# Who scales and rounds the ternary weights: six passes over 128x2048 moved from VectorE to GpSimd

## The reference

```python
weights = softmax(tokens @ gate_w); topk_w, topk_idx = top_k(weights, 2)
e0 = silu(x @ w0.T + b0);  e1 = silu(x @ w1.T + b1)
out = e0 * topk_w[:, 0] * (topk_idx[:, 0] == 0) + e1 * topk_w[:, 1] * (topk_idx[:, 1] == 1)
```

```python
scale = 1.0 / clip(mean(abs(w)), 1e-05)
wq = clip(round(w * scale), -1.0, 1.0) / scale
```

## Time and profile before

| what | value |
| --- | --- |
| median of 3 runs | 1935.88 us (1935.24 to 1936.64) |
| the profiled execution | 1937.66 us, of which the span of the trace is 1935.7 us |
| mean granted TensorE clock of that execution | 0.971 of full speed |
| busy shares of the span | PE 93%, DVE 73%, ACT 53%, POOL 26% |

### The profile page before, as it was taken

One profiled execution on the slowest core, in us unless ns is written; L12 is line 12 of the kernel. 1 busy time (PEld: TensorE's weight loads), 2 busy tenths in 40 slices (PEclk: granted clock), 3 DMA queues, 4 the chain that ended last, 5 costly groups with the idle time before them and its releaser, 6 DMA issues. The chain is left out here.

```text
span 1935.7 us, 33792 instructions
## 1 busy us (share of the span) xinstructions
PE 1793.0 (93%) x11747; PEld 1585.4 (82%) x11750; DVE 1410.4 (73%) x3157; ACT 1020.4 (53%) x2247; POOL 507.4 (26%) x531
## 2 busy tenths in 40 slices
PE   7958999999999999999967999999969999999698
PEld 6637999999898989899845888888857888888587
DVE  6478787777777787778666566666777777777786
ACT  4344656555556555565535565556622666666421
POOL 0514030211203030302011233333441444343342
PEclk9978999999999999999988999999989999999799
DMA  4011000000000000000021112110000000000011
GB/s 160 1 77 33 2 4 9 2 10 0 11 0 11 0 12 0 3 0 1 1 98 49 53 58 64 47 64 14 9 1 17 15 9 23 9 10 4 23 56 40
DMA packets 17591, 48.43 MB, mean 25 GB/s; under 512 B 2602, under 2 KB 7347, under 8 KB 15796
## 3 DMA queue, kind: packets, MB, share of 16 engines
q1 hardware_dynamic: 16596, 45.99, 7.3%
q10 hardware_dynamic: 864, 0.83, 0.1%
HBM read 45.89 MB, written 0.92 MB: 24 GB/s over the span
## 5 line engine op out<-in xcount | busy, mean ns | idle before, releaser
L1280 ACT ACTIVATE a_pH<-banks 125x512 fp32r<-125x512 f32 (+1 forms) x384 | 203.9, 544 | 273.6 <-PE banks L195 192.2
L1351 DVE TENSOR_TENSOR a_pL<-banks,a_pH 125x512 fp32r<-125x512 f32 (+1 forms) x384 | 235.2, 623 | 100.3 <-ACT a_pH L1280 96.6
L1854 POOL TENSOR_TENSOR a_prob<-a_prob,a_rinv 112x750 f32<-112x750 f32 x128 | 184.1, 1438 | 395.9 <-DVE a_rinv L2157 395.9
L1327 DVE TENSOR_SCALAR_CACHE_REDUCE a_prob<-banks 128x500 f32<-128x500 f32 x336 | 223.1, 677 | 18.0 <-PE banks L195 9.0
L1181 PE MATMUL banks<-ident,a_prob 128*125 128x128 f32 x1344 | 201.6, 274 | 6.6 <-ACT a_prob L1265 4.4
L195 PE MATMUL banks<-a_pH,a_head_vH 125*128 125x256 f32 (+1 forms) x576 | 203.2, 353 | 2.1 <-DVE a_pL L1351 1.1
L1265 ACT ACTIVATE a_prob<-a_prob,a_nmax 128x1000 f32<-128x1000 f32 x168 | 188.0, 1122 | 28.2 <-DVE a_nmax L1330 28.2
L1181 PEld LDWEIGHTS banks<-ident,a_prob 128*125 128x125 f32 x1344 | 187.1, 188 | 10.0 <-ACT a_prob L1265 4.9
L1137 POOL TENSOR_TENSOR a_head_oH<-a_o,ones 128x256 fp32r<-128x256 f32 (+1 forms) x24 | 16.5, 687 | 625.5 <-DVE a_o L1360 625.5
L195 PE MATMUL banks<-a_pH,a_head_vL 125*128 125x256 f32 (+1 forms) x576 | 173.0, 300 | 0.0
L195 PE MATMUL banks<-a_pL,a_head_vH 125*128 125x256 f32 (+1 forms) x576 | 172.8, 300 | 0.0
(11 more groups left out here) (422 smaller groups left out, 5094.9 us busy)
## 6 DMA issues: line engine op xcount, KB each, us to landing
a_w_out<-in_f_out SPq DMA_DIRECT2D x6, 1024.0 KB, 4.8
a_w_in<-in_f_in SPq DMA_DIRECT2D x12, 512.0 KB, 4.7
f_raw<-in_f_w SPq DMA_DIRECT2D x9, 513.0 KB, 3.6
pair_qk_raw<-in_a_qk SPq DMA_DIRECT2D x16, 256.0 KB, 2.7
f_quant_raw<-in_f_w SPq DMA_DIRECT2D x3, 1024.0 KB, 7.5
a_head_w_raw<-in_a_w SPq DMA_DIRECT2D x8, 384.0 KB, 3.0
a_v<-in_ctx_rows SPq DMA_DIRECT2D x4, 576.0 KB, 7.5
f_w_out<-in_f_out SPq DMA_DIRECT2D x2, 1024.0 KB, 5.1
```

The lines of the kernel that those rows point to most:

```text
L1280: act.activation(pH[:, c % RING, 0:wide], TB[c % 4][0:KB, 0:wide], ACT.Copy).then_inc(t_high, 1)
L1327: dve.tensor_scalar(prob[:, at, c * CHUNK:(c + 1) * CHUNK], SB[c % 3][:, 0:CHUNK], SCALE, None, ALU.mult, ALU.max, accum_out=chunk_max[:, ...
L1351: dve.tensor_tensor(pL[:, c % RING, 0:wide], TB[c % 4][0:KB, 0:wide], pH[:, c % RING, 0:wide].bitcast(F32), ALU.subtract).then_inc(t_done, 1)
L1854: pool.tensor_tensor(both, both, rinv[:, n % RING, :].unsqueeze(2).to_broadcast([SEQ, 2, KEYS]), ALU.mult).then_inc(p_normed, 1)
```

## The change

The six passes over `quant_raw` leave VectorE's loop and stand at the end of GpSimd's block of the same stage, as scale 0, round 0, scale 1, round 1, scale 2, round 2. Shapes, types, operations, semaphores and their counts are as before; ScalarE's and TensorE's blocks are not touched.

```diff
-        def quant_scale(dve, m):
-            dve.wait_ge(scale_ready, 1)
-            dve.tensor_scalar(quant_raw[:, m, :], quant_raw[:, m, :], w_scale[:, m:m + 1], 1.0,
+        def quant_scale(pool, m):
+            pool.wait_ge(scale_ready, 1)
+            pool.tensor_scalar(quant_raw[:, m, :], quant_raw[:, m, :], w_scale[:, m:m + 1], 1.0,
                               ALU.mult, ALU.min).then_inc(quant_scaled, 1)
...
-            dve.wait_ge(quant_scaled, m + 1)
-            dve.tensor_scalar(quant_raw[:, m, :], quant_raw[:, m, :], -1.0, MAGIC, ALU.max, ALU.add).then_inc(quant_clipped, 1)
+            pool.wait_ge(quant_scaled, m + 1)
+            pool.tensor_scalar(quant_raw[:, m, :], quant_raw[:, m, :], -1.0, MAGIC, ALU.max, ALU.add).then_inc(quant_clipped, 1)
...
             pool.wait_ge(w_cut, 1)
             pool.tensor_tensor(wL[:], w_raw[:], wH[:].bitcast(F32), ALU.subtract).then_inc(w_cut, 1)
+            for m in range(3):
+                quant_scale(pool, m)
+                quant_round(pool, m)
...
                     dve.reciprocal(w_scale[:], s.w_mean[:]).then_inc(scale_ready, 1)
-                if QUANT_AT < i <= QUANT_AT + 3:
-                    quant_scale(dve, i - QUANT_AT - 1)
-                if QUANT_AT + 1 < i <= QUANT_AT + 4:
-                    quant_round(dve, i - QUANT_AT - 2)
```

More of the change, by code:

```diff
@@ L710, in layer0_ffn, with quant_round @@
         EB = B[4:8]
-        def quant_scale(dve, m):
-            dve.wait_ge(scale_ready, 1)
-            dve.tensor_scalar(quant_raw[:, m, :], quant_raw[:, m, :], w_scale[:, m:m + 1], 1.0,
+        def quant_scale(pool, m):
+            pool.wait_ge(scale_ready, 1)
+            pool.tensor_scalar(quant_raw[:, m, :], quant_raw[:, m, :], w_scale[:, m:m + 1], 1.0,
                               ALU.mult, ALU.min).then_inc(quant_scaled, 1)
-        def quant_round(dve, m):
-            dve.wait_ge(quant_scaled, m + 1)
-            dve.tensor_scalar(quant_raw[:, m, :], quant_raw[:, m, :], -1.0, MAGIC, ALU.max, ALU.add).then_inc(quant_clipped, 1)
+        def quant_round(pool, m):
+            pool.wait_ge(quant_scaled, m + 1)
+            pool.tensor_scalar(quant_raw[:, m, :], quant_raw[:, m, :], -1.0, MAGIC, ALU.max, ALU.add).then_inc(quant_clipped, 1)
         block = ctx.enter_context(nc.Block())
```

## The result

| | median of 5 runs | range |
| --- | --- | --- |
| before | 1935.88 us | 1933.40 to 1938.09 |
| after | 1966.31 us | 1963.64 to 1970.99 |

The ratio is 1.0168, with a 95% interval of 1.0152 to 1.0183; of 1935.88 us that is 32.5 us more (29.4 to 35.4); the two medians as they stand are 30.4 us apart. The forecast was 2.6 us more, and its range ended at 1950. The profiled execution of the changed kernel took 1963.64 us, the lowest of its five.

What follows compares the result with a forecast made beforehand. The stage's end, ScalarE's last brought_back at 143.52, was taken as the bound; 134.9 + 6 d with d = 1.87 gave 146.1, so 1935.88 + 2.6 = 1938.5 us, range 1936.3 to 1950.

Steps and rivals of the forecast that it cites:

- The price of one pass, d: Length of each scale or round on GpSimd over 2048 columns: 1.87 us, range 1.87 to 4.45.
- GpSimd's loop is slower than a copy's: Rival, chance 0.38: the six GpSimd passes run well above 1.87 us each; 13.4 us later at 3.66, 18.1 at 4.45.
- The sum: Stage end at 134.9 + 6 d = 146.1 against 143.52, that is 6 d - 8.6 = 2.6 us later.
- the start: GpSimd's scale 0 starts at about 131.35, after the reciprocal ending at 130.95 and an addition ending at 131.31.
- the additions: VectorE's additions let in between GpSimd's passes, three at 0.5 us each, added to GpSimd's end.
- The reload: Library reload on GpSimd, in its idle stretch ahead of the six passes, put at nothing.
- The rival of the first call: Rival, chance 0.03: GpSimd's first pass behind the reload pays about 6 us for loading code, giving 1944.5 us.
- a sign of being wrong: The prediction called itself wrong if, among other signs, GpSimd's first pass was longer than the third.
- The lock: VectorE instructions with two SBUF operands stand still while GpSimd computes, entering only where GpSimd's next instruction waits for a semaphore.
- The cap on a gain: ScalarE's chain, ending at about 141.1 at best, limits any gain at the stage's end to 2.4 us or 0.12%.
- The tails: Behind GpSimd's last round: ScalarE's last brought_back to 146.05 and VectorE's four remaining additions to 146.15.

Runs made afterwards that it cites:

- prices: Kernel before plus a stage of its own with fifteen GpSimd instructions: multiply and add 1.90 us, multiply alone 5.4, multiply and minimum 7.09; its total time was not read.
- forms: Kernel before plus a stage of its own with GpSimd in other operation pairs, then small VectorE instructions beside GpSimd ones; rows read, not its time; addition stood 3.7 of 5.4 us.
- one_op: Changed kernel with one operation in each of the six passes, limits at -1 and 1 left out: 1959.67 us, ratio 1.0134.
- madd: Changed kernel with all six passes as multiply and add with plain numbers, so no ternary weights come out: 1936.50 us, ratio 1.0013.
- rounds_pool: Half of the change: VectorE keeps the three scales, GpSimd does only the three rounds: 1953.00 us, ratio 1.0098 against the kernel before.
- no_passes: Kernel before without the six passes on any engine, and brought_back not waiting for them: 1931.16 us, ratio 0.9982.
- fast_form: Change rebuilt: GpSimd multiplies by the scale and adds the rounding constant, VectorE takes maximum and minimum: 1937.22 us, ratio 1.0019 against the kernel before.
- spread: Kernel before rebuilt: scales on ScalarE and VectorE, VectorE writes bf16, no brought_back, maximum put off to GpSimd in layer 1's attention: 1931.55 us, ratio 0.9988.

## Why the prediction was wrong

- **The price of one pass, d, is the step that failed.** "It is nearest to the CAST, and I take 1.87; the ends for the range are 1.87 and 4.45." It measured 7.16 and 7.09, outside of both ends. The reason given, "as if reading set the pace and not the arithmetic", holds for the instructions of the earlier trace rows, and for no TENSOR_SCALAR but the pairs of multiply and add (prices, forms). The nearest rows were of other instructions; they bounded nothing, and the range should not have ended at them. The rival "GpSimd's loop is slower than a copy's" had the direction, with a chance of 0.38, but neither the size nor the reason: two operations are not slow as such, multiply and add take 1.90 us, and a factor per partition costs 0.07. The miss is 5.2 to 5.3 us a pass, six times.
- **What the Trainium skill made of it.** The Trainium skill (GPSIMD Engine Reference, section 3.1) gives 1.03 cycles an element for up to two operations. Against that, 7.16 us for 2048 elements are an estimate of 4.2 cycles, with the 1.2 GHz that the prediction took from the same reference. Only the fast form, 1.90 us, is near its figure. The measurement decides.
- **The sum held.** With the true d it gives 3 x (7.16 + 7.09) - 8.6 = 34.1 us, against 33.0 for the stage and 32.5 for the kernel. For one_op, with d = 5.4, it has 23.8 and the stage grew by 22.3; for madd, with d = 1.90, it has 2.8 and the stage grew by 1.9. So it is over by 1 to 1.5 us each time. In the changed kernel two terms account for it: the start, taken 0.4 us behind the reciprocal and measured at 0.1, and the additions, taken at 1.5 us. The six passes took 43.1 us from first start to last end where their lengths alone make 42.7.
- **Start and reload.** The first pass starts 0.10 us behind the reciprocal, with the addition beside it (7.32 instead of 7.16 us). The reload stands at 111.0, with 1 ns a record, in GpSimd's idle stretch: put at nothing, and was nothing. The rival of the first call is dead: that pass is 0.15 us longer than the third scale, not 6. By the letter of the prediction even this was a sign of being wrong. But being first is not the reason: in rounds_pool all three rounds took 7.24 us, in place of the 7.09 of a round in prices.
- **The lock.** "Stands still while GpSimd computes" is right for fast passes and for the first 4.5 us or so of a slow one of two operations; after that additions run beside it (from 134.61 in the timeline after, 2.4 us before the scale ends at 137.00). That VectorE gets in "where GpSimd's next instruction waits for a semaphore, not where GpSimd runs on" is wrong for the additions: in madd additions got in behind scales and rounds alike, and cost GpSimd about 0.1 us each, not 0.5. The row that this reading rested on, line 118 in the earlier trace rows, is of another kind than the additions: a TENSOR_SCALAR that reads one tensor and two numbers per partition. It hardly changed the sum: that term was 1.5 us. The Trainium skill (SBUF — State Buffer, "Who interferes with whom") speaks of a lock for a whole instruction; the length of the one-operand form, 7.09 us, agrees, the addition that stood 3.66 of 5.40 us doesn't.
- **The cap on a gain.** It was put at 2.4 us, and in no_passes the stage was 3.4 us shorter. The prediction added small gaps between ScalarE's instructions; they overlap by 0.1 us instead, and ran for 5.9 us from the SiLU of tile 5 to the end, not 6.5. At this d the cap played no part.
- **The tails.** Expected were two of equal length near 146. VectorE's was at 149.52, since ScalarE's `brought_back` of 144.20 held up the SiLU of tile 6, and ScalarE's at 174.76 alone.

## What to carry to other kernels

Before work goes to another engine, look for the very same instruction, with its pair of operations, in a trace of that engine; if there is none, a copy's row is a lower end and not an estimate (1.87 us here, against 7.16), and a run of that one instruction tells more than any reasoning. VectorE and GpSimd held each other up enough to act as one queue for much of this work: in fast_form three passes of 1.28 us left VectorE and cost it 4.7 us of standing. Slow passes are better put where an engine is idle for long and nobody waits, here in an attention of 837 us, than ahead of a barrier. Even so, the best of the kernels that compute everything, spread, gained 0.1%, with an interval that reaches to nothing.

## What the runs showed of the hardware

- GpSimd's TENSOR_SCALAR over 128x2048 fp32: 1.90 us for multiply and add or add and multiply (1.97 with a factor per partition), 5.36 to 5.44 for one operation alone, 7.08 to 7.15 for the other three pairs tried (multiply and minimum, maximum and add, multiply and subtract). One operation is thus dearer than two of the right kind.
- TENSOR_TENSOR took 3.60 us with a broadcast operand as with two full ones at 2048 columns, though in the earlier trace rows the two seemed to differ.
- A slow pass holds up a VectorE addition with two operands in SBUF for part of its time only (3.66 of 5.40 us, 4.54 of 7.09), but a one-operand TENSOR_SCALAR of VectorE for all of it (7.09 of 7.10). What changes inside the instruction after that part stays open.
